# A loop of six rounds over two steps, written out as twelve steps

## The reference

```python
# x: (16, 192, 32, 32); _gn: 32 groups, eps 1e-5
def ref(x, qkv_w, proj_w, proj_b):          # DIM 192, NUM_HEAD 6, DIM_HEAD 32
    xt = x.reshape(B, C, N).transpose(0, 2, 1)
    qkv = jnp.einsum('bnc,oc->bno', xt, qkv_w)
    qkv = qkv.reshape(B, N, 3, NUM_HEAD, DIM_HEAD).transpose(2, 0, 3, 1, 4)
    q, k, v = (qkv[0], qkv[1], qkv[2])
    attn = jnp.einsum('bhnd,bhmd->bhnm', q, k) * SCALE
    attn = jax.nn.softmax(attn, axis=-1)
    out = jnp.einsum('bhnm,bhmd->bhnd', attn, v)
    out = out.transpose(0, 2, 1, 3).reshape(B, N, C)
    out = jnp.einsum('bnc,oc->bno', out, proj_w) + proj_b
    return out.transpose(0, 2, 1).reshape(B, C, H, W)
x = x + ref(_gn(x), qkv_w, proj_w, proj_b)
```

## Time and profile before

| | |
|---|---|
| median of 3 runs | 1754.8 us (1754.24 to 1757.15) |
| the profiled execution's own time | 1756.06 us |
| its span, first to last instruction | 1754.3 us |
| instructions recorded | 30275 |
| PE busy | 1643.4 us, 94% |
| ACT, DVE, POOL busy | 1205.2, 1195.3, 1193.9 us (68 to 69%) |
| mean granted TensorE clock | 0.979 |
| DMA moved | 109.27 MB |

### The profile page before, as it was taken

The page is one execution under the profiler, slowest core; times in us unless marked ns, Lnnn a source line. Parts: engine busy times, 40 slices in busy tenths (PEclk is TensorE's granted clock), DMA queues, the critical chain, the costliest instruction groups (busy, mean ns, idle before and its releaser), DMA issues.

```text
span 1754.3 us, 30275 instructions
## 1 busy us (share of the span) xinstructions
PE 1643.4 (94%) x9440; PEld 540.4 (31%) x9440; DVE 1195.3 (68%) x2086; ACT 1205.2 (69%) x1969; POOL 1193.9 (68%) x581
## 2 busy tenths in 40 slices
PE   2689999999999999999999999999999999999992
PEld 1233333333333333333333333333333333233220
DVE  2487768676777767777686767768677777777710
ACT  1238686867768677776868767686867768677770
POOL 3126686786868658685867758586686868686882
PEclk9989999999999989999999989999999999999995
DMA  2404150331514123151503315140341513140202
GB/s 61 89 1 80 38 86 23 85 65 51 104 50 91 31 60 77 50 104 51 89 24 82 63 51 104 50 88 23 80 69 53 101 49 68 42 87 14 62 22 76
DMA packets 74284, 109.27 MB, mean 62 GB/s; under 512 B 26176, under 2 KB 39040, under 8 KB 74112
## 3 DMA queue, kind: packets, MB, share of 16 engines
q1 hardware_dynamic: 74112, 107.13, 28.7%
HBM read 42.99 MB, written 12.98 MB: 32 GB/s over the span
## 4 chain that ended last, share of the span: by engine, by line
PE 76%; POOL 6%; ACT 6%; issue 4%; DMA 1%; DVE 1%; SPq 0%; ACTq 0%; POOLq 0%; DVEq 0%
PE heads_ps L548 19%; PE max_ps L458 18%; PE scores_ps L533 17%; PE sums_ps L563 9%; ACT probs L676 4%; POOL prob_pairs L743 3%; PE extra_ps L516 2%; PE extra_ps L520 2%; PE extra_ps L517 2%; PE extra_ps L518 2%; PE extra_ps L521 2%; POOL xhat_b L711 1%; PE extra_ps L480 1%; POOL heads_out L720 1%; ACT xhat_b L631 1%
## 5 line engine op out<-in xcount | busy, mean ns | idle before, releaser
L817 DVE TENSOR_REDUCE half_max<-max_ps 128x1 f32<-128x512 f32 x1536 | 1012.6, 686 | 399.1 <-PE max_ps L458 385.3
L676 ACT ACTIVATE probs<-scores_ps,exp_scale 128x512 f32<-128x512 f32 x1536 | 993.3, 689 | 401.2 <-PE scores_ps L533 394.3
L743 POOL TENSOR_TENSOR prob_pairs<-probs 128x1024 f32<-128x1024 f32 x384 | 898.8, 2359 | 413.6 <-ACT probs L676 412.8
L533 PE MATMUL scores_ps<-q_stack,k_stack 98*128 98x512 f16 x1536 | 587.4, 384 | 25.9 <-issue 12.1
L458 PE MATMUL max_ps<-k_stack,q_stack 96*128 96x512 f16 x1536 | 595.1, 389 | 8.1 <-DVE half_max L817 5.3
L548 PE MATMUL heads_ps<-probs,v_sb 128*32 128x512 f32 x3072 | 413.5, 610 | 0.1
L458 PEld LDWEIGHTS max_ps<-k_stack,q_stack 96*128 96x128 f16 x1536 | 149.8, 98 | 580.8 <-issue 474.2
L533 PEld LDWEIGHTS scores_ps<-q_stack,k_stack 98*128 98x128 f16 x1536 | 150.2, 98 | 200.9 <-ACT probs L676 116.8
L563 PE MATMUL sums_ps<-prob_pairs,ones 128*32 128x512 f32 x1536 | 204.5, 604 | 1.1 <-POOL prob_pairs L743 1.1
L548 PEld LDWEIGHTS heads_ps<-probs,v_sb 128*32 128x32 f32 x3072 | 60.6, 108 | 140.5 <-issue 137.1
L870 DVE TENSOR_TENSOR qk_lo<-extra_ps,qk_hi 128x512 f16<-128x512 f32 x96 | 66.1, 688 | 48.3 <-ACT qk_hi L606 48.3
(11 more groups left out here) (92 smaller groups left out, 1028.1 us busy)
## 6 DMA issues: line engine op xcount, KB each, us to landing
q_stack<-qk_hi SPq DMA_DIRECT2D x96, 128.0 KB, 4.3
k_stack<-qk_hi SPq DMA_DIRECT2D x96, 128.0 KB, 5.5
inv_sb<-inv_rows SPq DMA_DIRECT2D x48, 256.0 KB
x_res<-x SPq DMA_DIRECT2D x16, 768.0 KB, 5.7
out<-x_res SPq DMA_DIRECT2D x16, 768.0 KB, 4.6
x_sb<-x SPq DMA_DIRECT2D x16, 512.0 KB, 6.9
x_sb<-x SPq DMA_DIRECT2D x32, 256.0 KB, 8.3
q_stack<-qk_lo SPq DMA_DIRECT2D x48, 128.0 KB, 4.2
```

The source lines that it names most:

```text
L533: pe.matmul(scores_ps[:, u_bank(s, u), :], k_stack[0:SHIFTED, st.parity, h, P * tile:P * (tile + 1)], q_stack[0:SHIFTED, st.parity, h, HAL ...
L676: nc.scalar.activation(probs[:, a, s % RING, HALF * half:HALF * (half + 1)], scores_ps[:, u_bank(s, u), :], ACT.Exp, scale=exp_scale[:, 0: ...
L743: nc.gpsimd.tensor_tensor(prob_pairs[:, a, j % PAIR_RING, :], probs[:, a, (s - 1) % RING, :], probs[:, a, s % RING, :], ALU.add).then_inc( ...
L817: nc.vector.tensor_reduce(half_max[:, a, tile, half:half + 1], max_ps[:, bank, :], AX_X, ALU.max).then_inc(max_read[bank], 1)
```

## The change

The loop is taken out of `run_steps`, and steps -3 to 16 are all written out. So every step's image number and count of extras are constants, and so are all waits' values. `due` and one condition on SP lose their case for an expression. The five calls of `run_steps` lose their first argument.

```diff
-LOOP_FIRST, LOOP_END = 1, 13
-
-
-def run_steps(eng, step):
+def run_steps(step):
 
     extras = 0
-    for at in range(-3, LOOP_FIRST):
+    for at in range(-3, BATCH + 1):
         st = Step(at, at, extras)
         step(st)
         extras = st.ordinal(SLOTS)
-    per = Step(LOOP_FIRST, LOOP_FIRST, 0).ordinal(SLOTS)
-    with eng.Fori(0, (LOOP_END - LOOP_FIRST) // 2) as i:
-        for k in range(2):
-            step(Step(2 * i + (LOOP_FIRST + k), LOOP_FIRST + k, 2 * per * i + (extras + per * k)))
-    extras += per * (LOOP_END - LOOP_FIRST)
-    for at in range(LOOP_END, BATCH + 1):
-        st = Step(at, at, extras)
-        step(st)
-        extras = st.ordinal(SLOTS)
 
 
 def due(count):
 
-    return not isinstance(count, int) or count > 0
+    return count > 0
...
-                    if s == LOAD_SLOT and st.project_in and not (isinstance(b, int) and b + 3 >= BATCH):
+                    if s == LOAD_SLOT and st.project_in and b + 3 < BATCH:
...
-            run_steps(pe, step)
+            run_steps(step)
```

More of the change, by code:

```diff
@@ L429, in step @@
                                      x_res[:, :, :]).then_inc(y_stored, MOVE)
-            run_steps(sp, step)
+            run_steps(step)
             sp.wait_ge(y_stored, MOVE * (BATCH + 1))
@@ L682, in step @@
                             between(st, s, u)
-            run_steps(act, step)
+            run_steps(step)
         @block.gpsimd
@@ L745, in step @@
                                                     probs[:, a, s % RING, :], ALU.add).then_inc(pairs_added, 1)
-            run_steps(pool, step)
+            run_steps(step)
         @block.vector
@@ L898, in step @@
                                                 AX_X, ALU.max, negate=True).then_inc(neg_max_ready, 1)
-            run_steps(dve, step)
+            run_steps(step)
 def u_bank(s, u):
```

## The result

| | kernel before | changed kernel |
|---|---|---|
| median, first comparison | 1755.97 us (4 runs) | 1730.67 us (1727.5 to 1732.86, 4 runs) |
| ratio | | 0.9849, 95% interval 0.9822 to 0.9876 |
| median, second comparison | 1754.74 us (7 runs) | 1730.79 us (1729.05 to 1731.19, 4 runs) |
| ratio | | 0.9865, 0.9847 to 0.9883 |
| profiled execution, its span | 1756.06, 1754.3 us | 1730.58, 1728.5 us |

The change makes the kernel 24 to 25 us faster; 25.1 were forecast, and 1729.7 us. The profiled executions differ by 25.5 us. The ratios are those on record; the quotient of two medians can differ from them by some 0.0007.

A forecast was written before the change was run, and what follows sets the result against it. The prediction took the kernel to be bound by PE, busy 1643.4 of 1754.3 us. Its terms 13.1 + 8.8 + 3.2 = 25.1 us, off the median of 1754.8, gave 1729.7 us, range 1727 to 1734.

The forecast's parts named there:

- (1): At the loop's round boundaries: PE's five jumps back, with the idle time each leaves on PE, go away, 13.1 us.
- the sentence on the other engines: At the jumps, ACT and DVE wait for PE and end no later, so nothing of theirs remains without PE's stall.
- (2): Behind the second and fourth jump: stretches at 1.2 in place of 2.4 GHz, taken as the stall's consequence, go, 8.8 us.
- rival B: Behind the jumps: the clock dips are not the stall's and stay, giving 1738.5 us; chance 0.05.
- The prediction's evidence against B: From 1240 to 1700 us: full clock throughout, in what was called 460 us of straight code at the end.
- (3): In the 12 loop steps: working out wait values in registers delays POOL and ACT, 0.27 us a step, 3.2 us.
- Rival A: The 0.27 us a step comes from step 13's missing statistics or load, not from registers: 1732.9 us; chance 0.08.
- Rival C: At rounds' starts: PE's idle time is not the jump and stays; only 3.6 us gained, 1751.2 us; chance 0.03.
- D: In the straight code: PE stalls 2.5 us in each of 12 steps for late instruction blocks, 1759.7 us; chance 0.04.

The follow-up runs named there:

- e1: Kernel before with only PE keeping the loop of six rounds, the other engines written out as straight code: 1752.53 us against 1757.42 before, ratio 0.9973.
- e3: Kernel before with the same loop on all engines, plus a prefetch hint for the branch at the top of each round: 1738.72 us against 1757.42, ratio 0.9889.
- e5: Kernel before with only ACT keeping the loop, the other engines straight code: 1752.36 us against 1754.51, ratio 0.9989.
- e2: Kernel before with only PE written out as straight code, ACT, DVE, POOL and SP keeping the loop: 1752.43 us against 1757.42, ratio 0.9969.
- e8: Kernel before with all engines looping three rounds over four steps in place of six over two: 1740.55 us against 1754.51, one run.
- e7: Changed kernel (no loop) with 38 unread semaphore increments on PE at the start of steps 3, 5, 7, 9 and 11: 1767.47 us, ratio 1.0072 to kernel before.
- e10: Changed kernel (no loop) with 30 unread semaphore increments on PE at the start of steps 3, 5, 7, 9 and 11: 1763.05 us, ratio 1.0041 to kernel before.
- e4: Kernel before with only POOL keeping the loop, the other engines straight code: 1735.21 us against 1757.42, ratio 0.9878.
- e9: Only ACT keeps the kernel before's loop, its first body instruction placed at the start of an instruction block: 1736.58 us against 1755.42, ratio 0.9888.

## Why the prediction was right, and where it was incomplete

(1) Five jumps back, 13.1 us: all five idle times are gone. e1 shows that PE makes them alone, e3 that it is the fetch at the target. Incomplete was the sentence on the other engines. That nothing of theirs remains holds for this change, which straightens all of them. But ACT's jumps alone cost as much as PE's (e5 against e1), and the two are paid once when both loop, because ACT's fetches pass while PE stands. In the trace of before three packets of instructions on q14 start between 407.0 and 410.0 us, and PE's array does nothing from 407.4 on the earlier trace rows. The 13.1 us are therefore no price of PE's code: straightening PE alone gains 0.3% (e2). Nor is the 45 ns of ACT's branch the price of its jump, as the prediction took it to be. In the trace of before the first instruction behind the taken branch comes 2.5 to 2.9 us after it on ACT (558 recorded instructions in the body) and 3.0 to 3.1 on DVE (414), against 0.24 to 0.31 on POOL (177) and SP (142), and e8 shows that POOL too pays 2.7 us once its body is longer. ACT's second fetch leaves no mark of its own there, since ACT was idle "for PE" anyway.

(2) Two stretches at half clock, 8.8 us: both are gone, and e7 and e10 show the cause without a loop, so rival B falls. The prediction's evidence against B was less than it said: of the 460 us up to 1700 only those from 1429 on are straight code; the rest is the last round of the loop, without a taken branch. How many there are varies by execution: two in the profile of before, five in e2, e5 and e7. Of the 19 runs of before beside e1 the fastest, 1750.77 us, has a mean granted clock of 0.981 and the slowest, 1760.96, of 0.974. The changed kernel's runs in both comparisons lie within 5.4 us. I read that as varying numbers of such stretches; the runs were not profiled one by one. The 8.8 us were taken from a single execution that happened to have two, so that the sum met the median this closely is in part luck.

(3) The arithmetic of the waits' values, 3.2 us: the steps came out at 99.75 us as forecast, and e4 and e5 split the 0.27 us into 0.18 on POOL and 0.10 on ACT. Rival A falls with the changed kernel's steps 1 to 12, which have both the statistics and the load.

Rival C falls with the changed kernel, e3 and e8, and D with the changed kernel too: straight code shows no new stop, twice over. The span came out at 1728.5 us, 0.7 under the 1729.2 that the sum gave, 0.44 of it ahead of step 1 (206.49 against 206.93), which the change does not touch.

## What to carry to other kernels

Find the branch in each engine's queue and look at the first instruction behind it: here an engine with a body of up to 280 recorded instructions went on 0.3 us after its jump, and one with 349 or more paid a fetch of 2.4 to 4.2 us. The fetches of ACT and DVE were hidden behind PE's stop. Undo them together, or the next one takes the first one's place. A stop of 2 to 4 us on PE cost up to 5.3 us of clock on top of its own length, and comparing one disturbed step with an undisturbed one in the same trace gives both prices before anything is built. It gives them for all engines together, not for one.

## What the runs showed of the hardware that was not expected

- ACT stopped a second time, for 2.3 to 2.6 us behind four of its five jumps, twelve recorded instructions behind its loop's head; moving the head to a block's start took that away and 16 us with it (e5, e9).
- POOL's jump, nearly free with a body of 177 recorded instructions, held it for 2.7 to 2.8 us with one of 349 (e4 against e8).
- A hint makes a taken branch cheap (3774 to 346 ns on PE) and is followed by a stop of 6.52 us on ACT behind the loop's end (e3).
- Needless semaphore increments on PE's queue start 0.151 us apart, and 38 of them in each of five places made this kernel slower than the loop did (e7, 1767.47 against 1754.51 us).
